# The transposes of split queries and keys in a fused four-layer block, from transpose operations to float32r products with the identity

## The chip, the cores and the metric

The kernel runs on one core of a Trainium2 chip. The metric is the time of one execution on the device in microseconds (us); the median of several executions counts.

## The reference

The input x has 32 sequences of 256 rows and 128 columns, float32. Four steps follow each other, each added to x:

1. attention with 16 heads of 8 columns on the layer norm of x, scaled by 1/sqrt(128), no mask;
2. a feed-forward net 128 to 512 to 128 with relu on the layer norm;
3. attention with 16 heads of 8 columns on the layer norm, with rotary positions, a causal mask, the scale 1/sqrt(8) and an output projection;
4. two layers of local attention (8 heads of 64 columns, window 64, normed queries and keys, rotary positions with a decay), each with a gated net of 341 hidden columns.

The change concerns steps 1 and 3 alone. Cut to what matters there:

```python
q = (x @ Wq.T).reshape(B, S, H, hd).transpose(0, 2, 1, 3)
k = (x @ Wk.T).reshape(B, S, H, hd).transpose(0, 2, 1, 3)
scores = jnp.einsum('bhqd,bhkd->bhqk', q, k) / jnp.sqrt(jnp.float32(D))
attn = jax.nn.softmax(scores, axis=-1)
out = jnp.einsum('bhqk,bhkd->bhqd', attn, v)
```

## The kernel before, in words

**Streams and passes.** Four streams work on four sequences at different stages: ATTN0 (steps 1 and 2), ATTN1 (step 3), LOCAL0 and LOCAL1 (the two layers of step 4). `stream_units` lists the units of each stream, such as "turn_q" or "scores". The strings in `TURNS` give for each engine, by hand, from which stream it takes its next unit, so the order of work on every engine is written out and fixed. A pass is one walk through such a string. Passes at the start and the end leave out streams without a sequence; the passes between them are one hardware loop with the same instructions each time. PSUM has two rings of four banks: "dense" and "score". Semaphores tell when a bank is filled and emptied.

**Split queries and keys.** The scores of the 16-head attentions are made from float32r operands. To keep their precision, the queries and keys are split: ScalarE rounds the value from PSUM to float32r (lines 656 and 657), and VectorE writes the rest, also as float32r (lines 832 and 833). QB and KB have 32 columns per head, of which 16 hold the high part twice, 8 the low part, and 2 (in QB) the negative maximum of the row, again in two parts (lines 851 and 853). A score is then the sum of products of parts over these 32 rows.

**The transposes.** The unit "turn_q" (two parts) takes QB, 128 rows of the sequence by 4 heads x 32 columns, and turns it with TensorE's transpose (line 1017) into a bank of the dense ring. A unit makes four transposes: two groups of heads times two halves of the sequence. ScalarE copies the bank into qT as float32r (line 663). "turn_k" does the same with KB; ScalarE copies to kS (line 668), and SyncE then issues four DMAs that place each head at its 32 partitions of kT (line 508). Line 1020 and after ("maxes") makes scores of all rows against all keys, from which VectorE takes row maxima (line 844). Then QB gets the maxima, and "turn_q" runs again ("with maxima"). "scores" (line 1053) makes the transposed scores, less the maximum, with float32r products of 128x128 stationary by 256 moving columns; ScalarE takes the exponential (line 680), and "mix" (line 1072) multiplies by V. Per sequence and attention, that is two units of queries, two of keys, two of queries with maxima: 24 transposes.

**The identity.** `ident_r` is a float32r tile [128, 128]; `ident` is the same memory seen as float32. `mm` is TensorE's matmul, `turn` its transpose. Masks are added by float32r products with `ident_r` (lines 1036, 1043, 1133, 1141). Plain float32 products are line 1108 (512 columns), 1135, 1172, 1180 and others. Other transposes (lines 994, 1080, 1118, 1151 to 1153) use `turn` with `ident` too.

Of the kernel before, what the change touches and what calls it, by code (L numbers as in the profile page):

```python
# [7 lines left out]
BATCH, SEQ, DIM = 32, 256, 128  # L8
STREAMS = 4
P = 128  # L10
# [260 lines left out]
def fused_block(nc, x, wqkv0, w1_0, b1_0, w2_0, b2_0, wqkv1, wo1, wqkv2, q_scale, k_scale, wo2,  # L271
                ln_g, ln_b, w1_2, b1_2, w2_2, b2_2, c_ident, c_masks, c_rope1, c_rope2, out):
    f32, f32r = mybir.dt.float32, mybir.dt.float32r
# [5 lines left out]
    with ExitStack() as ctx:  # L279
        def sb(name, shape, dt=f32):  # L280
            return ctx.enter_context(nc.sbuf_tensor(name, shape, dt))
# [8 lines left out]
        ident_r = sb("ident_r", [P, P], f32r)  # L290
        ident = ident_r[:].bitcast(f32)
# [79 lines left out]
        h = [probs[k][1][:, 0:TT * DIM].rearrange("p (t d) -> p t d", t=TT) for k in range(2)]\  # L371
# [65 lines left out]
        def tile(ring, u, n=0):  # L437
            return psum[ring][u.buffers[ring][n][0]]
# [4 lines left out]
        def has_filled(ring, u, n=0):  # L443
            return full[ring][u.buffers[ring][n][0]]
# [516 lines left out]
        def _(pe):  # L961
# [5 lines left out]
            mm, turn = nc.tensor.matmul, nc.tensor.transpose  # L967

            def unit(u, pas, j):
                k, l = u.stream, u.stream - LOCAL0  # L970
# [5 lines left out]
                if u.kind in ("turn", "shift"):  # L976

                    needs = [free("dense", u)]
                    if u.kind == "turn":
                        src = h[k]  # L980
# [4 lines left out]
                    else:  # L985
                        src = Y[l]
# [6 lines left out]
                    for t in range(TT):  # L993
                        last = turn(tile("dense", u)[:, t * P:(t + 1) * P], src[:, t, :], ident)
                    last.then_inc(has_filled("dense", u), 1)
                elif u.kind == "qkv":
                    t = u.part
# [4 lines left out]
                elif u.kind in ("turn_q", "turn_k"):  # L1002
                    src = QB if u.kind == "turn_q" else KB
# [10 lines left out]
                    for e in range(2):  # L1014
                        g = 2 * u.part + e
                        for t in range(TT):
                            last = turn(tile("dense", u)[:, e * SEQ + t * P:e * SEQ + (t + 1) * P],  # L1017
                                        src[:, k, t, 4 * g:4 * g + 4, :].rearrange("p h c -> p (h c)"), ident)
                    last.then_inc(has_filled("dense", u), 1)
                elif u.kind == "maxes":  # L1020
                    needs = [free("score", u)]
# [4 lines left out]
                    n, e = u.part // 2, u.part % 2  # L1026
# [3 lines left out]
                    if k == ATTN0:  # L1030
                        t, g = n // 4, n % 4
                        last = mm(bank, qT[:, k, g, t * P:(t + 1) * P], kT[:, k, 4 * g + 2 * e:4 * g + 2 * e + 2, :],  # L1032
                                  start=True, stop=True)
                    elif n < 2:
                        g = 2 * n + e
                        mm(bank, ident_r[:], causal.unsqueeze(1).broadcast_to([P, 4, P]), start=True, stop=False)
                        last = mm(bank, qT[:, k, g, 0:P], kT[:, k, 4 * g:4 * g + 4, 0:P], start=False, stop=True)
                    else:

                        g = n - 2  # L1040
                        mm(bank, qT[:, k, g, P:SEQ], kT[:, k, 4 * g + 2 * e:4 * g + 2 * e + 2, :], start=True, stop=False,
                           skip_group_check=True)
                        last = mm(bank.rearrange("p (a k) -> p a k", a=2)[:, :, P:SEQ], ident_r[:],
                                  causal.unsqueeze(1).broadcast_to([P, 2, P]), start=False, stop=True, skip_group_check=True)
                    last.then_inc(has_filled("score", u), 1)
                elif u.kind == "scores":

                    g, t, e = u.part // 4, u.part % 4 // 2, u.part % 2
# [3 lines left out]
                    for i in range(2):  # L1052
                        last = mm(tile("score", u)[:, i * SEQ:(i + 1) * SEQ], kT[:, k, 4 * g + 2 * e + i, t * P:(t + 1) * P],  # L1053
                                  qT[:, k, g, :], start=True, stop=True)
                    last.then_inc(has_filled("score", u), 1)
                elif u.kind == "mix":

                    g = u.part
# [4 lines left out]
                    for t in range(TT):  # L1063
# [7 lines left out]
                        for n in range(4):  # L1071
                            last = mm(tile("dense", u)[32 * n:32 * n + 16, q0:SEQ], V[:, k, t, 4 * g + n, :],  # L1072
                                      probs[k][t][:, n * w:(n + 1) * w], start=t == 0, stop=t == 1)
                    last.then_inc(has_filled("dense", u), 1)
                elif u.kind == "attn_out":
                    t = u.part
                    for sem, count in newest(pas, j, *of("mix", *range(GROUPS)), free("dense", u)):
                        pe.wait_ge(sem, count)
                    for g in range(GROUPS):
                        last = turn(tile("dense", u)[:, g * P:(g + 1) * P], oT[:, k, g, t * P:(t + 1) * P], ident)  # L1080
                    last.then_inc(has_filled("dense", u), 1)
                elif u.kind == "project1":
                    for sem, count in newest(pas, j, *of("turn"), free("dense", u)):
                        pe.wait_ge(sem, count)
                    for t in range(TT):
                        last = mm(tile("dense", u)[:, t * P:(t + 1) * P], hT[k][:, t * P:(t + 1) * P], wo1_sb[:], start=True, stop=True)
                    last.then_inc(has_filled("dense", u), 1)
                elif u.kind == "up0":
                    for sem, count in newest(pas, j, *of("turn"), free("dense", u)):
                        pe.wait_ge(sem, count)  # L1090
                    for e in range(2):
                        c = 2 * u.part + e
                        last = mm(tile("dense", u)[:, e * SEQ:(e + 1) * SEQ], w1_0_sb[:, c * P:(c + 1) * P], hT[k],
                                  start=True, stop=True)
                    last.then_inc(has_filled("dense", u), 1)
                elif u.kind == "down0":
                    for sem, count in newest(pas, j, *of("up0", 0, 1), free("dense", u)):
                        pe.wait_ge(sem, count)
                    for t in range(TT):
                        for c in range(FF0 // P):  # L1100
                            last = mm(tile("dense", u)[:, t * P:(t + 1) * P], up0T[:, c, t * P:(t + 1) * P], w2_0_sb[:, c, :],
                                      start=c == 0, stop=c == FF0 // P - 1)
                    last.then_inc(has_filled("dense", u), 1)
                elif u.kind == "qkv2":
                    t, m = u.part // 3, u.part % 3
                    for sem, count in newest(pas, j, *of("shift"), free("dense", u)):
                        pe.wait_ge(sem, count)
                    mm(tile("dense", u)[:], hS[:, l, t * P:(t + 1) * P], wqkv2_sb[:, l, m * INNER:(m + 1) * INNER],  # L1108
                       start=True, stop=True).then_inc(has_filled("dense", u), 1)
                elif u.kind in ("turn_q2", "turn_k2"):  # L1110
                    src = q2 if u.kind == "turn_q2" else k2
# [3 lines left out]
                    for e in range(2):  # L1115
                        pr = 2 * u.part + e
                        for t in range(TT):
                            last = turn(tile("dense", u)[:, e * SEQ + t * P:e * SEQ + (t + 1) * P],  # L1118
                                        src[:, l, t, pr * P:(pr + 1) * P], ident)
                    last.then_inc(has_filled("dense", u), 1)  # L1120
                elif u.kind == "scores2":
# [5 lines left out]
                    n, e = u.part // 2, u.part % 2  # L1127
# [3 lines left out]
                    if n == 0:  # L1131

                        mm(bank, ident_r[:], band0.unsqueeze(1).broadcast_to([P, 4, P]), start=True, stop=False)
                        for pr in (2 * e, 2 * e + 1):
                            last = mm(bank[:, (pr - 2 * e) * SEQ:(pr - 2 * e + 1) * SEQ], qT2[:, l, pr, 0:P],  # L1135
                                      kT2[:, l, pr, :, 0:P], start=False, stop=pr == 2 * e + 1)
                    else:
# [4 lines left out]
                        last = mm(two, qT2[:, l, pr, P:SEQ], kT2[:, l, pr, :, WINDOW:SEQ], start=False, stop=True)  # L1142
# [11 lines left out]
                elif u.kind == "mix2":  # L1154
# [6 lines left out]
                    for q0, w, t, c0 in ((0, P + WINDOW, 0, 0), (P, P, 1, P + WINDOW)):  # L1161
                        for e in range(2):
                            hd = 2 * n + e
                            last = mm(tile("dense", u)[64 * e:64 * e + 64, q0:q0 + w], V2[:, l, t, hd * HD:(hd + 1) * HD],  # L1164
                                      probs2[l][n % 2][:, e, c0:c0 + w], start=t == 0, stop=t == 1, skip_group_check=True)
                    last.then_inc(has_filled("dense", u), 1)
                elif u.kind == "project2":
                    for sem, count in newest(pas, j, *of("mix2", *range(PAIRS)), free("dense", u)):
                        pe.wait_ge(sem, count)
                    for t in range(TT):  # L1170
                        for c in range(PAIRS):
                            last = mm(tile("dense", u)[:, t * P:(t + 1) * P], o2T[:, l, c, t * P:(t + 1) * P], wo2_sb[:, l, c, :],  # L1172
                                      start=c == 0, stop=c == PAIRS - 1)
                    last.then_inc(has_filled("dense", u), 1)
                elif u.kind == "up2":
# [3 lines left out]
                    for half in range(2):  # L1179
                        last = mm(tile("dense", u)[0:n, half * SEQ:(half + 1) * SEQ],  # L1180
                                  w1_2_sb[:, l, half * HID + at:half * HID + at + n], hT[k], start=True, stop=True)
                    last.then_inc(has_filled("dense", u), 1)
                elif u.kind == "down2":
                    for sem, count in newest(pas, j, *of("up2", 0, 1, 2), free("dense", u)):
                        pe.wait_ge(sem, count)
                    for t in range(TT):
                        for c, (at, n) in enumerate(HTILES):
                            last = mm(tile("dense", u)[:, t * P:(t + 1) * P], up2T[0:n, l, c, t * P:(t + 1) * P], w2_2_sb[0:n, l, c, :],
                                      start=c == 0, stop=c == 2)
                    last.then_inc(has_filled("dense", u), 1)  # L1190

            run(pe, "tensor", unit)


# [31 lines left out]
```

## Time and profile before

| What | Value |
|---|---|
| median of 3 runs | 3539.75 us (3533.16 to 3548.29) |
| profiled execution, its own time | 3529.4 us |
| its span from first to last instruction | 3527.7 us |
| TensorE products busy | 3059.9 us, 87% of the span, 20480 records |
| TensorE weight loads busy | 2171.1 us, 62%, 20480 records |
| VectorE busy | 2544.7 us, 72% |
| ScalarE busy | 2226.6 us, 63% |
| GpSimd busy | 1580.9 us, 45% |
| mean granted TensorE clock | 0.967 of full |

The profile is of one execution. PE is TensorE with its products (a busy PE can be waiting in its pipeline, since products overlap), PEld its weight loads, DVE VectorE, ACT ScalarE, POOL GpSimd, SP SyncE. The time from one product's start to its end contains the way through the array; the rate in a stream is the distance from start to start. A merged row of x8 spans from the first start to the last end. The "chain" follows the work back from the last instruction to what released it.

### The profile page before, as it was taken

The page shows a single profiled execution, that of the slowest core. Times are in us where ns is not written, and L with a number is a line of the kernel's source. Part 1 is how long each engine was busy: PE and PEld are TensorE (multiplying, and loading weights), DVE is VectorE, ACT ScalarE, POOL GpSimd, SP SyncE. Part 2 cuts the span into 40 slices and gives each one's busy share as a digit, 9 for nine tenths or more (in the row PEclk, how much of TensorE's full clock was granted, in tenths as well). Part 3 has the DMA queues.
Part 4 walks back from the last instruction along what each step waited for, and adds up shares of the span by engine and source line. Part 5 has one row for each costly group of instructions (what it writes and reads, how often), then busy time and mean ns, then how long its engine had stood idle before and what let it go on. Part 6 is the DMA issues. An engine that isn't in the chain of part 4 may idle for free.

```text
span 3527.7 us, 69696 instructions
## 1 busy us (share of the span) xinstructions
PE 3059.9 (87%) x20480; PEld 2171.1 (62%) x20480; DVE 2544.7 (72%) x5886; ACT 2226.6 (63%) x6084; POOL 1580.9 (45%) x1741
## 2 busy tenths in 40 slices
PE   4678999999999999999999999999999999988764
PEld 2455666666666666666666666666666666665543
DVE  3466777877877778778777787787777877866543
ACT  2345767666666676666666676666666766665532
POOL 1034444555544445555444455554444555544432
PEclk8799999999999999999999999999999999999877
DMA  2000100111110001111100011111000111100000
GB/s 66 20 20 21 24 22 23 28 27 25 25 28 22 21 22 28 27 24 26 28 22 21 22 28 27 24 26 28 22 21 22 28 27 23 28 22 16 16 14 10
DMA packets 113412, 85.69 MB, mean 24 GB/s; under 512 B 27274, under 2 KB 112692, under 8 KB 113332
## 3 DMA queue, kind: packets, MB, share of 16 engines
q1 hardware_dynamic: 113332, 84.68, 10.5%
q8 instruction: 43, 0.70, 0.1%
q14 instruction: 37, 0.30, 0.0%
HBM read 9.17 MB, written 4.19 MB: 4 GB/s over the span
## 4 chain that ended last, share of the span: by engine, by line
PE 31%; issue 26%; DVE 20%; DMA 9%; ACT 5%; POOL 5%; SPq 2%; DVEq 1%; POOLq 0%; ACTq 0%
DMA V<-XY 4%; DMA kT<-rawP 4%; PE score L1053 4%; DVE negmax L844 3%; PE dense L1118 3%; PE dense L1164 3%; DVE rawP L911 2%; PE dense L1072 2%; DVE rawP L909 2%; DVE negmax L938 2%; PE dense L1108 2%; DVE P L948 2%; PE dense L1172 2%; PE dense L1180 2%; PE score L1151 2%
## 5 line engine op out<-in xcount | busy, mean ns | idle before, releaser
L844 DVE TENSOR_REDUCE negmax<-score 128x2 f32<-128x512 f32 (+1 forms) x896 | 558.0, 680 | 51.6 <-PE score L1032 25.3
L680 ACT ACTIVATE probs<-score 128x512 f32<-128x512 f32 (+1 forms) x1024 | 497.5, 554 | 135.0 <-PE score L1053 131.9
L604 POOL TENSOR_TENSOR rawQ<-rawQ,rawP 128x512 f32<-128x512 f32 x256 | 343.3, 1341 | 197.9 <-DVE rawP L911 192.9
L560 POOL TENSOR_TENSOR veps<-moments,eps_tile 128x2 f32<-128x2 f32 x192 | 37.4, 195 | 850.1 <-DVE moments L793 850.1
L580 POOL TENSOR_SCALAR_AFFINE_SELECT probs<-probs 128x256 f32<-128x256 f32 x512 | 217.1, 446 | 443.8 <-ACT probs L680 439.6
L1053 PE MATMUL score<-qT,kT 128*128 128x256 f32 x2048 | 380.2, 306 | 35.4 <-ACT probs L680 22.0
L1108 PE MATMUL dense<-wqkv_sb,hS 128*128 128x512 f32 x768 | 369.1, 612 | 18.6 <-DVE rawC L826 16.8
L609 POOL TENSOR_TENSOR rn<-ss,minus_half 128x16 f32<-128x16 f32 x128 | 373.1, 2914 | 13.3 <-DVE ss L918 13.0
L938 DVE TENSOR_REDUCE negmax<-score 128x2 f32<-128x384 f32 (+1 forms) x384 | 221.8, 596 | 215.0 <-PE score L1135 206.0
L1053 PEld LDWEIGHTS score<-qT,kT 128*128 128x128 f32 x2048 | 280.0, 191 | 117.8 <-issue 73.7
L710 ACT ACTIVATE rawP<-score,negmax 128x128 f32<-128x128 f32 x512 | 180.2, 370 | 194.3 <-DVE negmax L938 193.1
L663 ACT ACTIVATE qT<-dense 128x512 fp32r<-128x512 f32 x256 | 140.7, 606 | 223.3 <-PE dense L1017 223.3
L1072 PE MATMUL dense<-probs,V 128*16 128x256 f32 (+1 forms) x4096 | 247.0, 357 | 5.8 <-ACT probs L680 4.2
L695 ACT ACTIVATE rawP<-dense 128x512 f32<-128x512 f32 x256 | 152.7, 596 | 124.4 <-PE dense L1108 110.1
L1032 PE MATMUL score<-kT,qT 128*128 128x512 f32 x512 | 208.4, 482 | 25.2 <-DMA kT<-rawC 13.8
L1108 PEld LDWEIGHTS dense<-wqkv_sb,hS 128*128 128x128 f32 x768 | 137.0, 194 | 144.2 <-issue 119.3
L1180 PE MATMUL dense<-rawQ,w_sb 128*128 128x256 f32 (+1 forms) x768 | 198.6, 397 | 14.6 <-DVE KB L833 9.4
L601 POOL TENSOR_TENSOR rawQ<-rawB,rope_sb 128x512 f32<-128x512 f32 x128 | 166.7, 1302 | 99.4 <-DVE rawB L925 99.4
L710 ACT ACTIVATE P<-score,negmax 128x192 f32<-128x192 f32 x512 | 209.6, 449 | 1.2 <-DVE negmax L938 1.2
L1142 PE MATMUL score<-kT,rawQ 128*128 128x384 f32 x512 | 208.0, 488 | 0.0
L1017 PE MATMUL dense<-ident_r,QB 128*128 128x128 f32 x1024 | 140.5, 282 | 74.2 <-DVE QB L853 65.0
L1017 PEld LDWEIGHTS dense<-ident_r,QB 128*128 128x128 f32 x1024 | 118.0, 145 | 119.3 <-issue 89.1
(158 smaller groups left out, 7791.2 us busy)
## 6 DMA issues: line engine op xcount, KB each, us to landing
kT<-rawC SPq DMA_DIRECT2D x256, 128.0 KB, 2.5
kT<-rawP SPq DMA_DIRECT2D x128, 256.0 KB, 3.9
xin<-x SPq DMA_DIRECT2D x32, 128.0 KB, 2.1
out<-xout SPq DMA_DIRECT2D x32, 128.0 KB, 1.8
V<-Y SPq DMA_DIRECT2D x32, 63.5 KB
V<-XY SPq DMA_DIRECT2D x32, 63.5 KB
wqkv_sb<-wqkv SPq DMA_DIRECT2D x1, 1536.0 KB
w_sb<-w SPq DMA_DIRECT2D x1, 682.0 KB
```

Of the source, the lines that this page charges most:

```text
L580: nc.gpsimd.affine_select(out=part, in_=part, compare_op=ALU.is_ge, fill=0.0, base=0, pattern=[[0, 2], [1, P]], channel_multiplier=-1)\
L604: nc.gpsimd.tensor_tensor(cosine2[:, l, n, :], cosine2[:, l, n, :], two_in_P0[:, l, n, :], ALU.add)\
L609: nc.gpsimd.tensor_tensor(rn[:, l, t].rearrange("p m h -> p (m h)"), ss[:, l, t].rearrange("p m h -> p (m h)"), minus_half[:], ALU.pow).th ...
L680: nc.scalar.activation(dst, src, ACT.Exp, scale=SCALE0 if k == ATTN0 else SCALE1)\
L710: last = nc.scalar.activation(dst, src, ACT.Exp, bias=negmax[:, k, t, hd:hd + 1], accum_out=expsum[:, l, t, hd:hd + 1])
L844: nc.vector.reduce_max(negmax[:, k, t, h0:h0 + nh], tile("score", u)[:, :].rearrange("p (h k) -> p h k", h=nh), AX.X, negate=True).then_in ...
L938: nc.vector.reduce_max(dst, src, AX.X, negate=True).then_inc(sig("max_done", u), 1)
L1017: last = turn(tile("dense", u)[:, e * SEQ + t * P:e * SEQ + (t + 1) * P], src[:, k, t, 4 * g:4 * g + 4, :].rearrange("p h c -> p (h c)"), ...
L1053: last = mm(tile("score", u)[:, i * SEQ:(i + 1) * SEQ], kT[:, k, 4 * g + 2 * e + i, t * P:(t + 1) * P], qT[:, k, g, :], start=True, stop=True)
L1072: last = mm(tile("dense", u)[32 * n:32 * n + 16, q0:SEQ], V[:, k, t, 4 * g + n, :], probs[k][t][:, n * w:(n + 1) * w], start=t == 0, stop= ...
L1108: mm(tile("dense", u)[:], hS[:, l, t * P:(t + 1) * P], wqkv2_sb[:, l, m * INNER:(m + 1) * INNER], start=True, stop=True).then_inc(has_fill ...
L1180: last = mm(tile("dense", u)[0:n, half * SEQ:(half + 1) * SEQ], w1_2_sb[:, l, half * HID + at:half * HID + at + n], hT[k], start=True, sto ...
```

## The change

The four calls of `turn` in the units "turn_q" and "turn_k" of both 16-head attentions become `mm` with the source seen as float32r as the stationary operand and `ident_r` as the moving one. Shape, destination, order and semaphores stay as they are.

```diff
@@ -1014,8 +1014,9 @@
                     for e in range(2):
                         g = 2 * u.part + e
                         for t in range(TT):
-                            last = turn(tile("dense", u)[:, e * SEQ + t * P:e * SEQ + (t + 1) * P],
-                                        src[:, k, t, 4 * g:4 * g + 4, :].rearrange("p h c -> p (h c)"), ident)
+                            last = mm(tile("dense", u)[:, e * SEQ + t * P:e * SEQ + (t + 1) * P],
+                                      src[:, k, t, 4 * g:4 * g + 4, :].rearrange("p h c -> p (h c)").bitcast(f32r), ident_r[:],
+                                      start=True, stop=True)
                     last.then_inc(has_filled("dense", u), 1)
                 elif u.kind == "maxes":
                     needs = [free("score", u)]
```

## Rows read from the trace of the kernel before

**Rows 1.** The page: span, and busy time by engine

```profile
span 3527.7 us, 69696 instructions
PE 3059.9 (87%) x20480; PEld 2171.1 (62%) x20480; DVE 2544.7 (72%) x5886; ACT 2226.6 (63%) x6084; POOL 1580.9 (45%) x1741
```

**Rows 2.** The chain that ended last: start us, us, what

```profile
1015.43 4.82 DMA V<-XY
...
1116.21 4.83 DMA V<-XY
```

**Rows 3.** Windows, columns: us, busy PE, PEld, DVE, ACT, POOL, clock, DMA share, GB/s

```profile
1000.00:1100.80 100.80, 92.72 (x642) 66.25 (x641) 78.38 (x183) 69.33 (x191) 49.07 (x55) 1.00 0.11 25
2000.00:2100.80 100.80, 92.66 (x642) 66.21 (x640) 78.43 (x184) 69.31 (x191) 49.10 (x54) 1.00 0.11 25
0.00:335.00 335.00, 221.55 (x1271) 146.66 (x1272) 168.06 (x409) 126.85 (x306) 73.87 (x104) 0.84 0.12 32
335.00:3154.00 2819.00, 2590.93 (x17888) 1850.45 (x17887) 2192.63 (x5105) 1935.52 (x5307) 1367.99 (x1509) 1.00 0.11 25
3154.00:3528.00 374.00, 247.43 (x1322) 174.02 (x1322) 184.06 (x373) 164.24 (x472) 139.07 (x129) 0.83 0.06 15
```

**Rows 4.** Waits of TensorE in the period 1000 to 1100.8 us: total, times, longest

```profile
PE dense L1017 <- DVE QB L853: 2.1, 2, 1.5
...
PE score L1041 <- DVE negmax L844: 1.1, 1, 1.1
PE dense L994 <- DVE probs L808: 1.0, 1, 1.0
```

**Rows 5.** By line, whole run: duration ns min/median/max; last a group: busy us, mean ns

```profile
L1017 PEld LDWEIGHTS dense<-ident_r,QB x1024: 137/141/231, 32.6 to 3262.6; 128*128 128x128 f32 x171
L1017 PE MATMUL dense<-ident_r,QB x1024: 270/273/477, 32.6 to 3262.7; 128*128 128x128 f32 x171
...
L1017 PE MATMUL dense<-ident_r,KB x512: 272/273/421, 33.5 to 3235.2; 128*128 128x128 f32 x171
...
L1053 PEld LDWEIGHTS score<-qT,kT x2048: 186/189/338, 55.6 to 3303.4; 128*128 128x128 f32 x187
...
L1172 PE MATMUL dense<-wo_sb,rawB 128*128 128x128 f32 x1024 | 125.0, 275 | 1.3 <-DVE rawB L858 1.1 <-issue 0.2
```

**Rows 6.** Window of one period, line 1017 alone: us, PE busy, PEld busy, clock, DMA

```profile
1000.00:1100.80 100.80, 6.09 (x48) 5.26 (x48) 1.00 0.11 25
```

**Rows 7.** Timeline around the transposes with maxima: start us, us, engine, line, xcount

```profile
1045.15 1.09 PE L1017 MATMUL dense<-ident_r,QB 128*128 128x128 f32 x8 [0.61 <-DVE QB L853]
...
1066.66 1.06 PE L1017 MATMUL dense<-ident_r,QB 128*128 128x128 f32 x8 [1.50 <-DVE QB L853]
...
1067.46 0.78 PEld L1053 LDWEIGHTS score<-qT,kT 128*128 128x128 f32 x6
```

**Rows 8.** Timelines of short windows on TensorE: start us, us, engine, line, xcount

```profile
1018.37 1.04 PE L1017 MATMUL dense<-ident_r,QB 128*128 128x128 f32 x8
...
1045.15 0.20 PEld L1017 LDWEIGHTS dense<-ident_r,QB 128*128 128x128 f32 x2 [1.24 <-issue]
...
1046.99 0.30 PEld L1053 LDWEIGHTS score<-qT,kT 128*128 128x128 f32 x2 [0.72 <-ACT qT L663]
...
1054.09 0.30 PEld L1053 LDWEIGHTS score<-qT,kT 128*128 128x128 f32 x2 [0.27 <-ACT probs L680]
...
1054.09 0.53 PEld L1053 LDWEIGHTS score<-qT,kT 128*128 128x128 f32 x4 [0.27 <-ACT probs L680]
...
1080.26 1.95 PE L1172 MATMUL dense<-wo_sb,rawB 128*128 128x128 f32 x16
...
1057.56 0.49 PE L1133 MATMUL score<-masks,ident_r 128*128 128x512 f32 x1 [1.19 <-DMA kT<-rawP]
...
1062.87 0.44 PE L1141 MATMUL score<-masks,ident_r 128*128 128x384 f32 x1 [0.40 <-ACT rawP L710]
```

## The prediction, made before the changed kernel ran

> **What bounds the kernel now.** I read the page first, then the steady stretch by windows, the waits of TensorE, and last single instructions on TensorE. The page shows a span of 3527.7 us in a profiled execution of 3529.4 us, TensorE's products busy 87% of it and no other engine above 72% [rows 1]. The steady part repeats every 100.8 us: the same DMA starts at 1015.43 and at 1116.21 [rows 2]. In one such period products are busy 92.7 us; the rows of 1000 and 2000 us agree to 0.1 us, and the granted clock is 1.00 there, that is 2.4 GHz [rows 3]. The other 8.1 us of the period are its waits, the longest 1.5 us [rows 3, 4]. So TensorE bounds the steady part, with short waits in between. From 335 to 3154 us the clock is 1.00; the 335 us before and the 374 us after have 0.84 and 0.83, and products are busy only two thirds of them [rows 3]. There other engines and latencies set the pace. What counts is therefore how long TensorE is held per transpose, more than how long one lasts.
>
> **What the change touches.** Line 1017 makes 1024 transposes of QB and 512 of KB, each a weight load and a product [rows 5], and 48 of them lie in a period [rows 6], in groups of eight (two units). The change replaces these 1536 products one for one: same 128x128 stationary data, same 128 moving columns of the identity, same PSUM region, same waits, same order. Nothing is added or moved on another engine or queue, and no DMA changes. Of the six groups in a period, four stand in dense stretches of TensorE work, and two start when VectorE has written the maxima (L853), behind a wait of 0.61 and 1.50 us [rows 7].
>
> **Term 1, the rate in a stream.** Eight transposes end 1.04 us after the first one starts, and one lasts 0.273: (1.04 - 0.273) / 7 = 0.1096 us each [rows 5, 8]. What holds them? Two loads of a transpose in a row span 0.20 us, with 0.141 for one, so the second starts 0.06 after the first: the load is short, and the 128 columns set the 0.11. A float32r load (line 1053) is another thing: 0.189 long, and two span 0.30, so 0.11 apart even at the head of a burst, in two bursts alike; four span 0.53, (0.53 - 0.189) / 3 = 0.114 [rows 5, 8]. So where the transpose has a quick load and a slow stream, the float32r product should have a quick stream and a slow load. The stream can be bounded by single products that stood alone: 512 columns in 0.49 us, 384 in 0.44 [rows 8], so 0.05 per 128 columns. 128 columns then stream in about 0.055 us, in the shadow of a load of 0.11. A plain float32 product of 128 columns with such a load is in the trace too: 16 of line 1172 take 1.95 us, (1.95 - 0.275) / 15 = 0.1117 each [rows 5, 8]. I take this value, since load and columns are nearest: 0.1117 - 0.1096 = +0.0021 us per transpose, 1536 x 0.0021 = +3 us of TensorE time. With the load as limit the bounds are 0.11, as two loads in a row show (no change), and the 0.118 of six loads of line 1053, (0.78 - 0.189) / 5 [rows 7]: +0.0086, or +13 us. Far below lies a product held by its columns alone (rival two), far above one held by two passes (rival one).
>
> **Term 2, latency of a group that TensorE waited for.** The first transpose after a wait ends 1.09 - 7 x 0.1096 = 0.32 us after it starts [rows 7]. A float32r product that stands alone would take 0.44 - 2 x 0.05 = 0.34 [rows 8]. The difference of 0.02 us, in 2 x 28 groups, is 1 us. I count nothing: the longer load and the shorter stream cancel.
>
> **Term 3, the ends of the run.** 1536 - 28 x 48 = 192 transposes lie there, about a third of the time at the lower clock (0.84 is 32% of the time at half rate) [rows 3]. A transpose lasted up to 0.477 us at worst [rows 5], and the columns would take half as long. At most 60 x 0.1 = 6 us less; as TensorE is one third idle there, I take 0 and keep -6 as a bound.
>
> **Sum.** Some 0.9 of a change in TensorE's time reaches the end in the steady part (it waits 8.1 of 100.8 us), so +3 stays +3. The profiled execution would take 3529.4 + 3 = 3532 us. The median of the runs, 3539.75, stands 10 us above that execution, so I forecast 3543. What hides the halved stream is the weight load; if that cover were gone, the case is the second rival.
>
> **Rival one, slower: the short float32r product streams as slowly as a plain float32 one.** All float32r products in the trace have 256 columns or more; none shows what 128 do. A plain float32 product is two records (512 products of line 1172 are 1024 records [rows 5]), so 2 x 0.11 = 0.22 us for 128 columns. If the chip treats the short float32r product in that way, each transpose costs 0.11 more, 48 x 0.11 = 5.3 us a period. After two pairs of groups TensorE waits 1.0 and 1.1 us for VectorE [rows 4], which could swallow up to 2.1 of it; 3.2 to 5.3 us times 28 is 90 to 148, and the ends give 0 to 20. The time would be 3630 to 3708, most likely 3655. It decides from a product time above the 0.11 of the load. Against it: the fall of 0.05 us per 128 columns between 512 and 384 shows no step. For it: the row nearest in columns, line 1172 with 128, pays two passes, and the rows that pay one begin at 256 columns, so a step between them would not be seen here; hence a chance of one in four. The Trainium skill (Perfetto Trace Analysis, "Transposes") asks for the transpose operation in place of a standard matmul, since a transpose skips the arithmetic. It gives no price; by it the change could only lose.
>
> **Rival two, faster: the load of the new products is as quick as that of the transposes.** Then a product costs about 0.057 us, 0.053 less, 48 x 0.053 = 2.5 us a period and 70 us over 28 periods. Groups that VectorE releases gain little, and some of the rest turns into waits for VectorE (78.4 us busy of 100.8 [rows 3]) and ScalarE, so 25 to 70 us: 3470 to 3515, say 3490. Against it: the loads of line 1053, which are 0.11 apart even where nothing else holds them [rows 8]. The Trainium skill (TensorE: Matmul & The Clock Gate, "Weight-path perf modes") says that fast weight load is on for 128 weights of any type but FP32. If float32r counted as another type, this rival would hold; the trace does not agree with that, its float32r loads last 0.189 against 0.141 for the transposes [rows 5].
>
> **Rival three: nothing changes in the machine**, because the compiled product is the same pair of instructions as the transpose before. The time would stay at 3540; it can't be told from the forecast.
>
> **How the numbers follow.** The forecast gets 0.59, its own range 3528 to 3562: the bounds -6 and +13 and some 8 us for runs and for waits that shift. Rival one 0.26, rival two 0.10, rival three 0.05. A measurement of this kernel can tell about 0.5%, some 18 us, from no change. Faster takes 0.08 from rival two. Slower takes 0.26 from rival one and 0.03 from the forecast, where the products come at 0.118 or more and waits add to it. The rest, 0.63, is within 0.5%. The range goes down to 3526, which leaves out rival two, and up to 3660, which takes in the lower half of rival one, so that about 2 in 10 stay outside.
>
> **What would show it.** In the profile of the changed kernel, line 1017 should still have 1536 records, loads of 0.19 us in place of 0.141, products of about 0.22 in place of 0.273 (0.055 less), and eight of them within 1.0 us of each other's start and end, starts 0.11 apart. The steady period should be 100.8 to 101.1 us. 3072 records, or starts 0.22 apart and a period of 104 us or more, show rival one; starts 0.06 apart and a period under 100 us, rival two. I would be wrong in the mechanism, even at the right time, if loads were quick and the columns still took 0.11. If the ACT copies behind these units (line 663) or the scores behind them waited noticeably longer, a latency that I set to nothing would be the cause.

## The result, and the profile after

The changed kernel takes 3574.16 us (median of 5 runs, 3570.84 to 3577.03), the kernel before in the same runs 3535.76 us. The ratio is 1.0098, 95% interval [1.0073, 1.0124]: 38 us slower, where 3543 us and no visible change were forecast. The time lies inside the stated range of 3526 to 3660 us, but above the forecast's own 3528 to 3562, and none of the recorded cases describes what happened.

First the page of the changed kernel and its mean granted clock, which answer to [rows 1].

```profile
span 3575.3 us, 69696 instructions
PE 3119.4 (87%) x20480; PEld 2236.6 (63%) x20480; DVE 2548.2 (71%) x5886; ACT 2232.4 (62%) x6084; POOL 1581.8 (44%) x1741
...
die 0 (median of its cores): 3575.3 us, clock 0.946
```

There are as many records as before, 20480, and no engine but TensorE has noticeably more work. TensorE's products are busy 60 us longer, and the mean clock is 0.946 against 0.967 before.

Next line 1017 by source (duration in ns min/median/max), the answer to [rows 5]. Then two groups of eight from timelines: one in a dense stretch, the answer to [rows 8], and the one behind the longest wait, the answer to [rows 7].

```profile
L1017 PEld LDWEIGHTS dense<-ident_r,QB x1024: 186/192/338, 33.1 to 3310.2; 128*128 128x128 f32 x171
L1017 PE MATMUL dense<-ident_r,QB x1024: 222/274/623, 33.1 to 3310.3; 128*128 128x128 f32 x171
...
928.68 1.18 PE L1017 MATMUL dense<-ident_r,QB 128*128 128x128 f32 x8
...
1077.99 1.08 PE L1017 MATMUL dense<-ident_r,QB 128*128 128x128 f32 x8 [1.50 <-DVE QB L853]
```

There is one record per product, and loads last 0.192 us in place of 0.141. Behind the longest wait eight products take 1.08 us where eight transposes took 1.06 [rows 7]. The dense group shown takes 1.18 us against 1.04 [rows 8]: its first record starts earlier, while the product before it still runs. A period without a low clock is no longer than before, as the next windows show. So the exchange is much as forecast, and by itself free.

Now windows of the changed kernel: a period without a low clock, the next period, a short window ahead of its low stretch, and the low stretch. The last line is the same short window of the kernel before, laid around its group of transposes behind the same wait. The columns are those of [rows 3].

```profile
895.80:996.60 100.80, 92.83 (x643) 66.68 (x642) 78.36 (x183) 69.33 (x191) 49.08 (x54) 1.00 0.11 25
996.60:1099.70 103.10, 95.74 (x642) 68.92 (x641) 78.76 (x183) 69.69 (x191) 48.92 (x54) 0.97 0.11 24
1076.00:1079.38 3.38, 1.88 (x18) 1.70 (x15) 3.28 (x9) 2.18 (x10) 2.73 (x2) 1.00 0.00 0
1079.38:1086.21 6.83, 6.53 (x31) 5.25 (x31) 5.95 (x8) 5.23 (x12) 5.37 (x5) 0.50 0.00 0
...
1064.67:1068.05 3.38, 1.88 (x19) 1.71 (x16) 3.28 (x9) 2.18 (x10) 2.73 (x2) 1.00 0.00 0
```

The first period lasts the same 100.8 us as before [rows 2]. The second lasts 103.1 us, and the whole difference comes with a stretch of 6.83 us at 0.50, that is 1.2 GHz. Just ahead of it products are busy for only 1.88 of 3.38 us: there is the wait of 1.50 us for the maxima, and behind it the group of eight products that now stream little. The kernel before has the same 1.88 of 3.38 us there, and its clock stays at 1.00. So the busy time of the records doesn't tell the two apart; what differs, as the experiments below test, is how much is streamed within it. The timeline of the changed kernel shows the work behind this place at the low clock.

```profile
1081.44 0.42 PE L1153 MATMUL score<-ident_r,P 128*128 128x128 f32 x1
1081.65 0.42 PE L1154 MATMUL score<-ident_r,P 128*128 128x128 f32 x1
...
1086.27 0.27 PE L1153 MATMUL score<-ident_r,P 128*128 128x128 f32 x1
1086.38 0.27 PE L1154 MATMUL score<-ident_r,P 128*128 128x128 f32 x1
```

Transposes of lines that were not changed start 0.21 us apart and last 0.42; later, with the clock back, 0.11 and 0.27.

How much does this explain? The low time is twice (1 - clock) times the span, 233 us before and 386 us after. By the granted clock in the traces, 113 of the 153 us more lie between 450 and 3090 us, in 26 low stretches of 3.4 or 6.8 us, where the kernel before has none. The other 40 lie at the two ends. The next two windows, first of the kernel before and then of the changed one, hold the same number of products in the steady part.

```profile
480.80:3102.40 2621.60, 2411.63 (x16642) 1722.38 (x16641) 2040.20 (x4758) 1801.71 (x4941) 1274.28 (x1405) 1.00 0.11 25
...
485.00:3147.80 2662.80, 2459.20 (x16643) 1776.11 (x16642) 2044.72 (x4758) 1807.52 (x4941) 1275.59 (x1404) 0.98 0.11 24
```

They take 2621.6 and 2662.8 us, 41 us more, or 0.37 us for each of the 113 low us. In the single period above it was 2.3 us for 6.83, or 0.34. The ends give the rest of the 48 us between the two spans.

The falls don't come in every period, though every period has the same instructions. Of the 26, 16 start within 3 us after ATTN0's group with maxima has started, the one behind the long wait, 5 as close behind ATTN1's group with maxima, and 5 some 10 us ahead of ATTN0's group, at the masks. What picks the periods was not tested.

### The profile page after: what moved, and what is told of

It is laid out like the page before. It is cut to its first block, busy times and chain, and to the rows that moved or that the text cites. A ratio compares the mean times of both kernels' runs of the same rounds, so it can differ in the third digit from the quotient of the medians.

```text
span 3575.3 us, 69696 instructions
## 1 busy us (share of the span) xinstructions
PE 3119.4 (87%) x20480; PEld 2236.6 (63%) x20480; DVE 2548.2 (71%) x5886; ACT 2232.4 (62%) x6084; POOL 1581.8 (44%) x1741
## 4 chain that ended last, share of the span: by engine, by line
PE 33%; issue 26%; DVE 19%; DMA 9%; ACT 5%; POOL 4%; SPq 2%; DVEq 1%; POOLq 0%; ACTq 0%
DMA V<-XY 4%; PE score L1054 4%; DMA kT<-rawP 4%; DVE negmax L844 3%; PE dense L1119 3%; PE dense L1165 3%; DVE rawP L911 2%; PE dense L1073 2%; DVE rawP L909 2%; PE dense L1109 2%; PE dense L1181 2%; DVE negmax L938 2%; PE score L1136 2%; PE score L1152 2%; PE dense L1017 2%
## 5 line engine op out<-in xcount | busy, mean ns | idle before, releaser
L1054 PE MATMUL score<-qT,kT 128*128 128x256 f32 x2048 | 396.7, 317 | 26.6 <-ACT probs L680 15.6
L1054 PEld LDWEIGHTS score<-qT,kT 128*128 128x128 f32 x2048 | 295.9, 201 | 109.1 <-issue 69.0
L1017 PE MATMUL dense<-ident_r,QB 128*128 128x128 f32 x1024 | 148.9, 290 | 80.9 <-DVE QB L853 67.9
L1017 PEld LDWEIGHTS dense<-ident_r,QB 128*128 128x128 f32 x1024 | 132.7, 199 | 124.6 <-issue 95.8
```

Of the source, the lines that this page charges most:

```text
L1017: last = mm(tile("dense", u)[:, e * SEQ + t * P:e * SEQ + (t + 1) * P], src[:, k, t, 4 * g:4 * g + 4, :].rearrange("p h c -> p (h c)").bit ...
```

## The experiments

The **clock theory** is that the float32r products give the array only half as long to stream in the same stretch of time, and that the granted clock falls behind the place where this meets a wait. Its rival, the **rate theory**, is that each new product is dearer in itself, so that the cost goes with their number. All ratios are against the kernel before in the same session.

**Which groups matter.** Two kernels split the 48 products of a period: first only those with maxima, then only the others.

```diff
+if u.source == "with maxima":      # second kernel: !=
     last = mm(..., src[...].bitcast(f32r), ident_r[:], start=True, stop=True)
+else:
+    last = turn(..., src[...], ident)
```

> Only the transposes of the queries with maxima (two groups of eight per period, each behind a wait of TensorE for VectorE) are float32r products; the other four groups stay transposes. Clock theory: the granted clock falls in the steady part because the array streams half as many column steps right behind such a wait; most falls of the changed kernel begin just behind these two groups, so most of them should stay: 0.955 mean clock or less, 1.0 to 2.0 low windows per period, time 3558 to 3574 us against 3536 before. Rate theory (the new products and their loads are themselves dearer and cost in proportion to their number): a third of the 38 us, 3549 us, with a clock like that of before.

> Only the four groups in dense stretches (first queries, and keys) are float32r products; the queries with maxima stay transposes. Clock theory: these groups have busy work on both sides, so the clock should hardly fall in the steady part: at most 0.3 low windows per period, mean clock 0.963 or more, time 3536 to 3546 us. Rate theory: two thirds of the 38 us, 3561 us, whatever the clock does.

The first took 3577.42 us, ratio 1.0121 [1.0103, 1.0139]; the second 3535.51 us, ratio 1.0002 [0.9992, 1.0013]. The first lies 3 us above the range of the clock theory and the second just under it, and both are far from the rate theory. A third of the products carries the whole loss, and two thirds cost nothing. The windows of the first, then of the second kernel:

```profile
335.00:3000.00 2665.00, 2472.75 (x16651) 1774.30 (x16650) 2045.83 (x4763) 1813.65 (x4946) 1275.29 (x1405) 0.98 0.11 24
```

```profile
335.00:3000.00 2665.00, 2450.28 (x16879) 1756.71 (x16878) 2076.66 (x4819) 1830.92 (x5020) 1297.92 (x1429) 1.00 0.11 25
```

The clock column and the instructions done in the same 2665 us (16651 against 16879 products) go together. The rate theory falls here.

**Which of the two groups with maxima.** The same edit for one attention alone.

```diff
+if u.source == "with maxima" and k == ATTN0:      # mirror: k == ATTN1
```

> One group of eight per period is float32r products: the queries with maxima of the first attention, which follow a wait of 1.5 us. In the run with both such groups every fall of the steady part began just behind this one. Clock theory, sharpened to one place: 24 of the 38 us or more stay with this one group alone, 3560 to 3578 us, mean clock 0.955 or less. Rival (both groups share in it, or the number of products counts): half of the loss or less, 3533 to 3553 us.

> The mirror of it: only the queries with maxima of the second attention (behind a wait of 0.6 us) are float32r products. Clock theory: no falls in the steady part beyond those of before, 3530 to 3542 us, mean clock 0.963 or more. Rival: like the other half, 3545 to 3560 us.

ATTN0 alone: 3572.79 us, 1.0107 [1.0091, 1.0124], clock 0.949. ATTN1 alone: 3536.08 us, 1.0011 [1.0001, 1.0020], clock 0.966. Eight products of 48, behind the longest wait of the period, are enough for the whole loss. The changed kernel without them:

```diff
+if u.source != "with maxima" or k == ATTN1:
```

> The changed kernel with only the queries with maxima of the first attention back as transposes: 40 of 48 float32r products per period stay. Clock theory: nearly all of the 38 us gone, 3533 to 3545 us. Rival (five groups of six keep their share): 3560 us or more.

It took 3538.74 us, 1.0016 [1.0006, 1.0025]. A small rest is left, and the trace has seven falls: four start some 10 us ahead of ATTN0's group, at the masks behind a wait for a DMA, and three of these are followed by one at the group itself.

**Same products, more streaming.** All 48 stay float32r products, but three of four stream the identity twice.

```diff
+at, w = e * SEQ + t * P, 1 if (e, t) == (1, TT - 1) else 2
-last = mm(tile("dense", u)[:, e * SEQ + t * P:e * SEQ + (t + 1) * P],
-          src[...].bitcast(f32r), ident_r[:],
-          start=True, stop=True)
+last = mm(tile("dense", u)[:, at:at + w * P].rearrange("p (a k) -> p a k", a=w),
+          src[...].bitcast(f32r),
+          ident_r[:].unsqueeze(1).broadcast_to([P, w, P]), start=True, stop=True)
```

> All 48 are float32r products as in the changed kernel, but three of four stream 256 columns of the identity (twice 128) in place of 128; the second half lands where a later product writes over it. Loads, their number and all waits stay. Clock theory: the array streams as long per load as the transposes did, so the falls in the steady part go: under 0.3 low windows per period, clock 0.963 or more, and since the load hides the longer stream, 3536 to 3550 us. Rate theory: the extra columns can only add, 3574 to 3590 us.

3539.27 us, 1.0014 [1.0002, 1.0025]. The timeline of the wide kernel at the group of ATTN0, then its windows:

```profile
1069.73 1.12 PE L1018 MATMUL dense<-ident_r,QB 128*128 128x256 f32 x8 [1.50 <-DVE QB L853]
...
335.00:3000.00 2665.00, 2459.40 (x16840) 1768.12 (x16842) 2075.96 (x4817) 1830.23 (x5015) 1300.16 (x1429) 1.00 0.11 25
```

The wait of 1.50 us is the same, and the eight products take 1.12 us against 1.08: the extra columns hide behind the loads almost wholly. Adding columns brought the ratio from 1.0098 down to 1.0014. The mean clock of the profiled execution, 0.959, is under the 0.963 that was expected, and seven short falls are left. So neither the float32r type nor the operation makes the clock fall, but how much is streamed.

**The wait filled.** The changed kernel, with three products of 512 columns in the free bank ahead of the wait for the maxima, in both attentions. The wait for the free bank, which the cut below leaves out, moves ahead of them.

```diff
+if u.part == 0:
+    for _ in range(3):
+        mm(tile("dense", u)[:], ident_r[:], kT[:, k, 0:2, :], start=True, stop=True)
 pe.wait_ge(sig("m_ready", u), so_far("m_ready", k, u, pas, j))
```

> The changed kernel with three float32r products of 512 columns (0.64 us) streamed into the free bank while TensorE would wait for the maxima, before each pair of units with maxima; their result is written over. Clock theory: the wait of 0.6 and 1.5 us that comes ahead of the thin products is filled, so falls behind these two groups go and those at the masks behind the DMA stay: 0.2 to 0.7 low windows per period, 3540 to 3560 us. Rate theory: work is only added, so 3574 us or more.

3540.22 us, 1.0019 [1.0009, 1.0028]. The timeline of this kernel:

```profile
1073.80 0.86 PE L1015 MATMUL dense<-kT,ident_r 128*128 128x512 f32 x3
1075.29 1.11 PE L1020 MATMUL dense<-ident_r,QB 128*128 128x128 f32 x8 [0.64 <-DVE QB L853]
```

The idle time shrinks from 1.50 to 0.64 us, and nearly all of the loss is gone although only useless work was added. That is better than was expected: two falls are left. It takes both, the wait and the thin products behind it.

**Without any float32r product.** Here the kernel before keeps its transposes, and four of the eight in the group of ATTN0 are left out.

```diff
-for t in range(TT):
+for t in range(1 if u.source == "with maxima" and k == ATTN0 else TT):
```

> The kernel before, all with transposes, but in the queries with maxima of the first attention those of the second half of the sequence are left out (four of eight; the output differs in these rows). The columns streamed there are halved, as by the change, with no float32r product in place. If what counts is how much the array streams around that wait: falls as in the run with this group changed, 3550 to 3578 us although work was removed. If what counts is that a product is not a transpose: no falls, and 0 to 0.44 us less per period, 3520 to 3536 us.

3537.72 us, 1.0018 [1.0008, 1.0028]. The forecast of 3550 to 3578 us missed. There are falls, at the same place, but nine in place of 26. The window of one of them, in a period of 102.1 us:

```profile
1070.00:1073.40 3.40, 3.02 (x15) 2.73 (x15) 3.40 (x5) 2.42 (x7) 1.94 (x3) 0.51 0.00 0
```

Work was removed, and the kernel did not get faster. But the group had also become some 0.4 us shorter, so that dense work came sooner, which may be why there are fewer falls. The next kernel nearly keeps the length of the group: four of the eight become products of 16 columns, and the kernel leaves out the rest of their output.

```diff
+if u.source == "with maxima" and k == ATTN0 and t == 1:
+    last = mm(tile("dense", u)[:, e * SEQ + t * P:e * SEQ + t * P + 16],
+              src[...].bitcast(f32r), ident_r[:, 0:16], start=True, stop=True)
```

> The kernel before; in the queries with maxima of the first attention the four transposes of the first half of the sequence stay, and the four of the second half become float32r products of 16 columns (the output differs in these rows). Their loads keep TensorE for about 0.11 us each while next to nothing streams, so the group lasts about as long as before with half its column time, as in the changed kernel. In the run that left these four out altogether the group was also 0.44 us shorter, and only every third period had a fall. If little streaming over an equal stretch is what makes the clock fall: a fall in every period or every second one, 3558 to 3578 us. If it takes all eight as products: 3533 to 3545 us.

3572.12 us, 1.0105 [1.0081, 1.0128], the full loss. The timeline of this kernel at the group, then the window of the fall behind it:

```profile
1074.29 0.30 PE L1022 MATMUL dense<-ident_r,QB 128*128 128x128 f32 x1 [1.51 <-DVE QB L853]
1074.35 0.26 PE L1018 MATMUL dense<-ident_r,QB 128*128 128x16 f32 x1
1074.46 0.33 PE L1022 MATMUL dense<-ident_r,QB 128*128 128x128 f32 x1
...
1076.10:1082.90 6.80, 6.19 (x29) 5.21 (x30) 5.91 (x8) 4.69 (x11) 5.34 (x6) 0.51 0.00 0
```

Four full transposes and four products that stream almost nothing, spread over the time of the group, do what eight float32r products do. From the start of the group to the next instruction it is 0.76 us here (1074.29 to 1075.05), 0.82 in the kernel before (1066.66 to 1067.48) and 0.92 in the changed one (1077.99 to 1078.91). So the loss doesn't come from a group that holds TensorE longer. This is the case that the theory names: little streaming per time over the stretch, whatever the instructions are.

**Can the low clock at the ends be won back?** Before and after the steady part the clock is low for some 230 us in the kernel before as well. This kernel fills waits there with products of 512 columns.

```diff
+def fill(ring, n):
+    if pas.times == 1:
+        for sem, count in newest(pas, j, free(ring, u)):
+            pe.wait_ge(sem, count)
+        for _ in range(n):
+            mm(tile(ring, u)[:], ident_r[:], causal.unsqueeze(1).broadcast_to([P, 4, P]), start=True, stop=True)
...
+fill("dense", 4)      # units "turn" and "shift"
+fill("dense", 3)      # first "turn_q" with maxima
+fill("score", 6)      # first "maxes", first "scores2"
+fill("score", 4)      # first "turn_p"
```

> The kernel before with float32r products of 512 columns streamed into free banks ahead of TensorE's waits, only in the passes before and after the steady part, where the clock is low for some 230 us in all; their results are written over. If the low clock costs time there as it does in the steady part, with products busy two thirds of the time: 3490 to 3528 us. If other engines and latencies set the pace there, or the added products come in the way: 3532 to 3560 us.

3548.28 us, 1.0038 [1.0025, 1.0050]: slower, as the second case expected, though the mean clock rose to 0.977. The window of its start, where before had a clock of 0.84 [rows 3]:

```profile
0.00:335.00 335.00, 247.57 (x1411) 167.16 (x1412) 166.91 (x408) 127.08 (x305) 73.75 (x104) 0.89 0.12 32
```

So the higher clock bought no time at the ends. Whether it is worth nothing where other engines set the pace, or whether the added products took more than it gave, this run doesn't separate; it also has four falls in the steady part. No version tried beats the kernel before; the best of them, with only the four groups in dense stretches changed, is equal to it.

**Falls in all kernels.** Each trace has this many low stretches between 450 and 3090 us, some 26 periods:

| Kernel | Low stretches | Ratio |
|---|---|---|
| before | 0 | 1 |
| ATTN1 alone | 0 | 1.0011 |
| only the dense groups | 2 | 1.0002 |
| wait filled | 2 | 1.0019 |
| ends filled | 4 | 1.0038 |
| changed, without ATTN0's group | 7 | 1.0016 |
| wide products | 7 | 1.0014 |
| half of ATTN0's transposes left out | 9 | 1.0018 |
| changed | 26 | 1.0098 |
| thin products among transposes | 26 | 1.0105 |
| ATTN0 alone | 26 | 1.0107 |
| both groups with maxima | 26 | 1.0121 |

## Why the prediction was right or wrong

**The rate in a stream** (term 1) was right in substance. Loads last 0.192 us, the group behind the long wait takes 1.08 us, periods without a fall 100.8; the change in the four dense groups alone measures 1.0002. That the load takes the place of the columns as the limit was the mechanism forecast, and the wide kernel, with twice the columns in 1.12 us, bears it out. Some sizes were off: the products last 0.274 and not 0.22, and eight of them take more than 1.0 us. Perhaps a product's record covers a wait for its load too; no run tests that.

**The latency behind a wait** (term 2) was nearly right: 1.08 against 1.06. The next instruction comes 0.10 us later than before, but periods without a fall don't show it.

**The ends** (term 3) brought no gain. Outside the two long windows of the steady part the profiled executions take 906 us before and 912 us after, 6 us more, with 40 us more of low clock. Each is one execution.

**The sum** is the step that failed. It says that "what hides the halved stream is the weight load", and gives that no price. The clock of 1.00 in the steady part was read from [rows 3] and taken as given, though it depends on how much TensorE streams, and this is just what the change halves. The missing term is 38 us, more than ten times the sum that was made. In its place the runs showed 26 falls of the clock behind halved streaming next to waits, which cost 41 us in the steady part. Its place could be seen beforehand: the group behind the longest wait of the period [rows 7]. Its size could not: no row of the kernel before shows a fall in the steady part.

**The range** holds the time by luck. It was stretched to 3660 to take in the lower half of rival one, whose mechanism did not occur; the forecast's own range ended at 3562.

**Rival one** had the right sign and the wrong mechanism: 1536 records and not 3072, starts 0.11 apart and not 0.22. Its sentence from the Trainium skill (Perfetto Trace Analysis, "Transposes") points the right way, yet these runs don't show its reason at work: in a stream the new product is hardly dearer than the transpose, 1.08 against 1.06 us for eight. **Rival two** fell with the loads of 0.192 us. **Rival three** fell by the same loads: the instructions are others than before.

On the clock itself the Trainium skill (TensorE: Matmul & The Clock Gate, "Part 1: The HAM clock gate") says that the ratio follows how busy the array has been lately. The runs agree only if busy is taken as streaming. By the records, products were busy 1.88 of 3.38 us in both kernels, and the clock fell to 0.50 in one and stayed at 1.00 in the other. The same page ("Part 4: PE-mode transpose") says that transposes don't count as busy in the same way. Here the measurement decides against it for float32 transposes: when four full ones gave way to thin products in a group of nearly equal length, the clock fell in every period, and with full transposes it stayed at 1.00. So they count more than products that stream little.

## What to carry to other kernels

Before halving what TensorE streams behind a cover (a weight load, a wait), look for the longest idle time of the engine near it, and give the fall of the clock there a price of its own: here 0.3 to 0.4 us per low microsecond over the steady part. Exchange operations in the dense stretches first, and measure those next to waits separately. If a thin operation must stand behind a wait, columns that hide behind its load, or work in the wait, may cost less than the low clock.

## What the runs showed of the hardware that was not expected

**A transpose and a float32r product of the same block reach nearly the same rate from opposite limits.** The loads of transposes can start 0.06 us apart [rows 8], yet the transposes start 0.11 apart, so most likely their columns hold them; the product is held to 0.11 by its load. For the product, 256 columns cost almost the same as 128: 1.12 against 1.08 us for eight.

**The falls come back in step.** In the kernel with only the group of ATTN0 changed, the group starts at 1079.76, 1183.18, 1284.46 and 1387.94 us in four periods in a row. The first of these (the line is from a short window, which holds three of the eight products):

```profile
1079.76 0.52 PE L1018 MATMUL dense<-ident_r,QB 128*128 128x128 f32 x3 [1.50 <-DVE QB L853]
```

The periods are 103.4, 101.3 and 103.5 us. From 467 us on, long and short ones alternate through the whole steady part, with a low stretch of 6.8 us in one and 3.4 in the next. The low stretches start 102.4 us apart each time. In the kernel before, a period is 100.8 us and has no fall. So it may be that each fall shifts the work so that the next one comes at the same moment of the period, and that one group is enough for the loss of all six for this reason. No run tests it. The short low stretch costs 0.5 us and the long one 2.6, each against 100.8, that is 0.15 and 0.38 us per low microsecond. So the price also depends on the work that it meets.
